# State-space scan: gates in the output weights, D u and residual rows as TensorE products, copies on ScalarE

## The reference, cut to what matters

```python
h = _layernorm(x) * (1 + ca) + sa
xz = h @ W_in                       # halves: x_conv input, z
x_conv = silu(causal_conv(xz[:, :128]) + conv_b)      # "u" in the kernel
B_sel, C_sel, delta = split(x_conv @ W_xproj);  delta = softplus(delta)
state = exp(delta * A) * state + delta * B_sel * u    # 16 states a channel, over time
y = sum_n(state * C_sel)
y = y + x_conv * D_param
y = y * silu(z)
x = x + ga * (y @ W_out)            # ga: one row of 128 gates for each batch
```

## Time and profile before

| | |
|---|---|
| median of three runs | 1981.86 us |
| the profiled execution | 1981.38 us, its span 1979.6 us |
| mean granted clock of TensorE over the span | 0.908 of full |
| scan stage, first to last group's product | 1395.08 to 1643.64 us |
| busy over the span | PE 82%, DVE 61%, ACT 39%, POOL 65% |

### The profile page before, as it was taken

The page is one execution under the profiler, slowest core; times in us unless marked ns, Lnnn a source line. Parts: engine busy times, 40 slices in busy tenths (PEclk is TensorE's granted clock), DMA queues, the critical chain, the costliest instruction groups (busy, mean ns, idle before and its releaser), DMA issues. The chain is left out here.

```text
span 1979.6 us, 26522 instructions
## 1 busy us (share of the span) xinstructions
PE 1617.7 (82%) x9024; PEld 1115.1 (56%) x9024; DVE 1201.4 (61%) x2409; ACT 764.4 (39%) x1278; POOL 1288.5 (65%) x1091
## 2 busy tenths in 40 slices
PE   5799999999999999999999899998776765347670
PEld 3455656665567556676565787886333333236560
DVE  6876666667665666756661456664799997511124
ACT  2245444354443544434445333222866530102120
POOL 4588898789887898878888511100477775481516
PEclk7799999999999999999999999999988876577885
DMA  6223122112211222121210200000000002022213
GB/s 168 65 76 96 44 65 65 37 40 65 54 44 44 65 47 51 41 68 40 58 33 12 62 1 1 1 1 22 0 1 0 0 0 88 29 71 66 79 50 83
DMA packets 82740, 90.67 MB, mean 46 GB/s; under 512 B 12448, under 2 KB 52276, under 8 KB 82608
## 3 DMA queue, kind: packets, MB, share of 16 engines
q1 hardware_dynamic: 78512, 80.97, 16.6%
q0 software_dynamic: 4096, 8.02, 1.4%
HBM read 24.05 MB, written 14.68 MB: 20 GB/s over the span
## 5 line engine op out<-in xcount | busy, mean ns | idle before, releaser
L835 DVE CUSTOM_DVE_ANT_0 ring<-ring,mask 128x128 f32<-128x128 f32 (+7 forms) x512 | 383.8, 769 | 184.3 <-PE ring L697 183.8
L921 ACT ACTIVATE prob<-ring 128x512 f32<-128x512 f32 x576 | 315.2, 597 | 297.0 <-PE ring L712 293.2
L975 POOL TENSOR_TENSOR acc<-acc,prob 128x512 f32<-128x512 f32 x272 | 353.6, 1300 | 72.6 <-ACT prob L921 48.8
L728 PE MATMUL ps_o<-prob,v 128*64 128x256 f32 x2304 | 281.5, 386 | 4.2 <-issue 3.8
L697 PE MATMUL ring<-k,x 128*128 128x512 f32 (+3 forms) x768 | 249.6, 405 | 37.3 <-ACT prob L921 22.3
L711 PE MATMUL ring<-x,k 128*128 128x512 f32 x576 | 257.2, 447 | 25.0 <-DVE neg_m L835 15.7
L712 PE MATMUL ring<-x,k 128*128 128x512 f32 x576 | 229.1, 398 | 0.0
L697 PEld LDWEIGHTS ring<-k,x 128*128 128x128 f32 x768 | 136.4, 197 | 145.1 <-ACT prob L921 51.2
L728 PEld LDWEIGHTS ps_o<-prob,v 128*64 128x64 f32 x2304 | 154.0, 136 | 106.1 <-issue 38.4
L972 POOL TENSOR_TENSOR acc<-prob 128x512 f32<-128x512 f32 x144 | 184.1, 1279 | 7.9 <-ACT prob L921 6.6
L942 POOL TENSOR_TENSOR other<-other,sin 128x512 f32<-128x512 f32 x96 | 136.5, 1422 | 58.1 <-DVE other L814 57.6
(11 more groups left out here) (302 smaller groups left out, 3179.8 us busy)
## 6 DMA issues: line engine op xcount, KB each, us to landing
x<-other SPq DMA_DIRECT2D x256, 128.0 KB, 2.4
x<-rot SPq DMA_DIRECT2D x128, 128.0 KB, 2.4
slots_in<-zeros SPq DMA_DIRECT2D x2, 2048.0 KB, 8.7
slots_out<-wo SPq DMA_DIRECT2D x16, 256.0 KB
gate<-slots_in SPq DMA_DIRECT2D x11, 256.0 KB
e_w<-in_w SPq DMA_DIRECT2D x3, 704.0 KB, 6.7
x<-shift SPq DMA_DIRECT2D x128, 2.0 KB
first_h<-in_x SPq DMA_DIRECT2D x4, 512.0 KB, 4.9
```

The costliest lines, as they stand in the source:

```text
L728: mm = e.matmul(ps_o[s * D:(s + 1) * D, qb % 2 * 2 * P:(qb % 2 + 1) * 2 * P], v[g % 2][:, kb, :], prob[i % NPROB][:, s * 2 * P:(s + 1) * 2 ...
L835: e.tensor_tensor_reduce(ps, ps, mask_1[:, SEQ - n:SEQ], 1.0, -3.0 * NEG, ALU.add, ALU.min, neg_m[g % 2][:, c, h, qb % QPC:qb % QPC + 1]). ...
L921: e.activation(prob[i % NPROB][:, :], banks(("s2",) + key, BANK), ACT.Exp, scale=-1.0).then_inc(s2_exp.sem, 1)
L975: e.tensor_tensor(total[:, :], total[:, :], tile[:, :], ALU.add).then_inc(summed.sem, 1)
```

## The change

Two constants are made once on GpSimd: `w_gated`, the output weights times the gates for each batch, and `diag`, D_param on the diagonal of a 128x128 matrix. D*u is then added by products `diag` x u into `ps_y`, one for each half, ahead of the second fold sum of every batch. The output products use `w_gated`, and a product of the identity with x adds the residual rows in the same bank. ScalarE copies the bank to x. For batches 0 to 2 ScalarE copies `ps_y` to y and GpSimd multiplies by z as before; for batch 3 VectorE multiplies `ps_y` by z itself.

```diff
+        w_gated, diag = sb("w_gated", (P, BATCH, HID)), sb("diag", (P, P))
...
                 elif kind == "out":
                     b, n = key
-                    e.wait_ge(y_pool.sem, y_pool.at[key])
+                    e.wait_ge(gated_pool, 2)
+                    e.wait_ge(*y_made(key))
...
-                        mm = e.matmul(bank[:, j * HID:(j + 1) * HID], y[:, blk], w_out[:, :], start=True, stop=True)
+                        e.matmul(bank[:, j * HID:(j + 1) * HID], y[:, blk], w_gated[:, b, :], start=True, stop=False)
+                        mm = e.matmul(bank[:, j * HID:(j + 1) * HID], ident[:, :], x[:, b * TPB + n * 4 + j, :], start=False, stop=True)
...
                     if g == 0 and b:
-                        e.wait_ge(y_dve.sem, y_dve.at[b - 1, NC2 - 1])
+                        e.wait_ge(y_act.sem, y_act.at[b - 1, NC2 - 1])
+                    if g == 1:
+                        e.wait_ge(gated_pool, 2)
+                        for c in range(NC2):
+                            e.matmul(ps_y[c][:, :], diag[:, :], u[b % 2][:, c * BANK:(c + 1) * BANK], start=False, stop=False)
...                       # VectorE
-                elif kind == "y":
+                elif kind == "y" and key[0] == BATCH - 1:
...
-                        e.scalar_tensor_tensor(y[:, cc], u[b % 2][:, cc], dp[:, 0:1], ps_y[c][:, :], ALU.mult, ALU.add).then_inc(y_dve.sem, 1)
-                elif kind == "out":
...
-                    e.tensor_tensor(scaled[:, :, :], ps_w[turn[step] % 2][:, :].rearrange("p (j n) -> p j n", j=4),
-                                    gate_bc[:, b:b + 1, :].to_broadcast([P, 4, HID]), ALU.mult).then_inc(scale_dve.sem, 1)
+                        e.tensor_tensor(y[:, cc], ps_y[c][:, :], z[b % 2][:, cc], ALU.mult).then_inc(y_last.sem, 1)
...                       # ScalarE
-                        e.wait_ge(y_dve.sem, y_dve.at[b - 2, NC2 - 1])
+                        e.wait_ge(y_pe.sem, y_pe.at[b - 2, NG // SET - 1])
...
+                elif kind == "y" and key[0] < BATCH - 1:
+                    b, = key
+                    for c in range(NC2):
+                        if c < NC2 - 1:
+                            e.wait_ge(last_pe.sem, last_pe.at[b])
+                        else:
+                            e.wait_ge(y_pe.sem, y_pe.at[b, NG // SET - 1])
...
+                        e.activation(y[:, c * BANK:(c + 1) * BANK], ps_y[c][:, :], ACT.Copy).then_inc(y_act.sem, 1)
+                elif kind == "out":
+                    b, n = key
+                    tile = b * TPB + n * 4
+                    e.wait_ge(w_pe.sem, w_pe.at[step])
+                    e.activation(x[:, tile:tile + 4, :], ps_w[turn[step] % 2][:, :].rearrange("p (j n) -> p j n", j=4),
+                                 ACT.Copy).then_inc(add_act.sem, 1)
...                       # GpSimd
+            e.wait_ge(loaded, LATER * 16)
+            e.tensor_tensor(w_gated[:, :, :], gate_bc[:, :, :], w_out[:, :].rearrange("p (o n) -> p o n", o=1).to_broadcast([P, BATCH, HID]),
+                            ALU.mult).then_inc(gated_pool, 1)
+            e.tensor_scalar(diag[:, :], ident[:, :], dp[:, 0:1], None, ALU.mult).then_inc(gated_pool, 1)
...
-                elif kind == "out":
...
-                    e.tensor_tensor(x[:, tile:tile + 4, :], x[:, tile:tile + 4, :], scaled[:, :, :], ALU.add).then_inc(add_pool.sem, 1)
```

More of the change, by code:

```diff
@@ L1810, in selective_scan @@
         half = NG * P // 2
-        sel_in0, sel_in1, consts, a_exp, a_ready, sel_done, rstd_act, nmr_dve = (
-            sem(n) for n in ("sel_in0", "sel_in1", "const", "a", "a_neg", "sel", "rstd", "nmr"))
+        sel_in0, sel_in1, consts, a_exp, a_ready, sel_done, rstd_act, nmr_dve, gated_pool = (
+            sem(n) for n in ("sel_in0", "sel_in1", "const", "a", "a_neg", "sel", "rstd", "nmr", "gated"))
         x_norm = mark("x_norm")
         w_pe, x_pe, y_pe = mark("w_pe"), mark("x_pe"), mark("y_pe")
-        act, delta_dve, bu_dve, scan_dve, y_dve, scale_dve = (
-            mark(n) for n in ("act", "delta", "bu", "scan", "y", "scale"))
-        y_pool, du_pool = mark("y_pool"), mark("du")
+        act, delta_dve, bu_dve, scan_dve, y_act = (
+            mark(n) for n in ("act", "delta", "bu", "scan", "y"))
+        y_pool, y_last, du_pool = mark("y_pool"), mark("y_last"), mark("du")
         last_pe = mark("last_pe")
-        da_act, hc_pool, add_pool = mark("da"), mark("hc"), mark("add")
+        da_act, hc_pool, add_act = mark("da"), mark("hc"), mark("add")
         row_chain = Steps(nc, sems, "m_stats")
@@ L1851, in selective_scan @@
                 for c in range(NC2):
-                    for m in (y_dve, y_pool):
+                    for m in (y_act, y_pool) if key[0] < BATCH - 1 else (y_last,):
                         m.add(key + (c,))
             elif kind == "out":
-                scale_dve.add(key), add_pool.add(key)
+                add_act.add(key)
         def bank_read(step):
@@ L1864, in bank_read, with y_made @@
             return act.sem, act.at[past]
+        def y_made(key):
+            m = y_pool if key[0] < BATCH - 1 else y_last
+            return m.sem, m.at[key]
         def du_made(kind, b):
```

22 lines of the change are left out of this document (9 added, 13 removed).

## The result

The changed kernel takes 1984.69 us in the median of 19 runs (1982.80 to 1988.78), the kernel before 1981.86 in 19 beside it. The ratio is 1.0017, with a 95% interval of 1.0010 to 1.0024: 2.0 to 4.8 us slower, a difference that is clear of noise but small. The forecast was 1987, 5.4 more than before, in a range of 1976 to 1995.

What follows compares the result with a forecast made beforehand. VectorE sets the scan's pace while TensorE fills banks in time; after the change TensorE was to bound stretches. Terms 1.7 + 0.9 - 2.0 + 0.1 + 1.6 + 1.3 + 1.5 + 0.3 = +5.4 us: 1987, range 1976 to 1995.

Steps and rivals of the forecast that it cites:

- norm and outputs, groups 18 to 22: Batch 1's first groups: norm behind ScalarE's copies and doubled output products make TensorE the bound, 1.7 us later.
- norm and outputs, groups 34 to 38: Batch 2's first groups: the same delayed norm and doubled output products, 0.9 us later.
- batch 2's y and outputs (50 to 54): Batch 3's first groups, no norm behind the copies: VectorE's saved y sums and output steps gain 2.0 us.
- signs that I had named: Products of 18 to 22 and 34 to 38 wait 1 to 1.5 us; 26, 42 and 58 over 1 us each.
- ScalarE's place in the order: Batch ends: y copies delay norm, transposes and next fill; 1.30 us saved becomes 1.1 lost at 18, 0.3 at 34.
- Rival 3: Norm's hole on TensorE drops its clock for 4 to 8 us, adding about 3 us per batch: 1992; chance 0.22.
- Twice the output products: Output steps: identity products double TensorE's instructions, 2.1 us more a batch, so TensorE bounds groups 18 to 22 and 34 to 38.
- The diagonal: Two fp32 products ahead of each batch's second fold sum: costs of 0.1, 1.6, 1.3 and 1.5 us in batches 0 to 3.
- Rival 2: Added products hold TensorE's clock high; the diagonal costs 0.1, 0, -0.5 and 0.3: 1982.5 us; chance 0.18.
- The tail: End of the stage: 32 output instructions instead of 16, clock rising partway; last statistics 0.3 us later, bounds -0.5 and +1.5.
- Rival 1: VectorE keeps the pace in the scan stage: 7.4 us less and the tail's 0.3, 1974.8 us; chance 0.12.

Runs made afterwards that it cites:

- 1: Changed kernel with the y step of batches 0 to 2 placed behind the second norm and turn instead of ahead: 0.9975 of the kernel before.
- 7: Changed kernel with VectorE multiplying the PSUM sums by z for every batch, without ScalarE copies or GpSimd products of y: 0.9988 of the kernel before.
- 10: Kernel before with ScalarE copying ps_y to y in place of VectorE's step (u times D_param left out): 0.9987 of the kernel before.
- experiment 3: Changed kernel without the identity products of the output steps (residual rows left out): 0.9997 of the kernel before.
- 11: Kernel before with the identity products with x added to its output steps: 1.0005 of the kernel before.
- 2: Changed kernel without the products of the diagonal with u (u times D_param left out): 0.9997 of the kernel before.
- 5: Changed kernel run again without any edit, for a second trace: 1.0013 of the kernel before.
- 9: Kernel before run again without any edit, for a second trace: 1985.53 us in a single execution.
- experiment 8: Changed kernel with batch 3's y made as the others, ScalarE copying and GpSimd multiplying by z: 1.0016 of the kernel before.
- 4: Changed kernel with the diagonal's products moved from the second fold sum to ahead of the third sum's wait for GpSimd: 1.0011 of the kernel before.
- 6: Changed kernel with y behind norm and turn and the diagonal ahead of the third sum's wait: 0.9973 of the kernel before.
- 12: Changed kernel with y behind norm and turn, diagonal ahead of the third sum's wait, in batch 3 behind the first fold sum: 0.9956 of the kernel before.

## Why the prediction was right, and where its terms were off

The direction held, and the time lies well inside the range; the size came to about half: +5.4 forecast, +2.05 in the stage by the traces, +2.8 by the medians. The mechanism was the one named: work left VectorE, and its waits for fills in groups 2 to 63 rose from 8.95 to 19.31 us, 10.4 where I had said 12.5. VectorE was relieved of 6.4 us up to group 63's product (busy 227.1 us instead of 233.5), not of 7.4. Up to there the stage grew by 4.06 where the forecast had 5.1; the tail had the wrong sign. Step by step, in us of the stage:

| step | forecast | measured |
|---|---|---|
| diagonal, batch 0 | +0.1 | +0.1 |
| norm and outputs, groups 18 to 22 | +1.7 | +2.6 |
| diagonal, batch 1 (26) | +1.6 | +0.3 |
| third sum, batch 1 (30) | 0 | +0.2 |
| norm and outputs, groups 34 to 38 | +0.9 | +0.3 |
| diagonal, batch 2 (42) | +1.3 | -0.4 |
| third sum, batch 2 (46) | 0 | +0.2 |
| batch 2's y and outputs (50 to 54) | -2.0 | -1.9 |
| diagonal, batch 3 (58) | +1.5 | +2.6 |
| tail | +0.3 | -2.0 |

Term by term the misses add up to 8.4 us, more than the whole difference, and they cancel down to 3.4. So the mechanism of the first step was foreseen, but that the sum came out near is in part luck: the terms that depend on TensorE's clock missed either way. Of the signs that I had named, the waits at 18, 34 and 58 came, those over 1 us at 26 and 42 did not (0.36 and 0.37).

**ScalarE's place in the order** was right and is shown by experiments 1, 7 and 10. Its size in batch 1's groups was that of the walk (1.1) plus the low clock behind the hole: 2.2 at group 18. Rival 3 named this, and its mechanism happened in one batch of two. Read in windows of half a microsecond, the granted clock is 1.00 from 1469.00 to 1472.00, 0.77 from there to 1472.50 and 0.50 until it rises again in the window 1475.50 to 1476.00: 3.4 us low, where the rival had 4 to 8, so that it cost 1.1 and not 3. In batch 2's groups the clock stayed high through the same hole, and the product came 0.26 later where I had 0.3.

**Twice the output products** bound TensorE where I said (waits at 20, 21 and 37 that experiment 3 takes away, and that are not there in 11, where VectorE kept its work), but the stretch cost 0.4 and 0 more after group 18 and 34, not 0.6 each.

**The diagonal** is the term that was mis-sized in batches 1 and 2: I let its products and the sum behind them run at the clock that the earlier trace rows show, 3.4 plus 1.9. They ran high, 1.98 and 1.92 (1.91 of the first before the second could start, where I had 1.7):

```profile
1502.39 1.98 PE L1959 MATMUL m_ps_y<-m_u,m_diag 128*128 128x512 f32 x4 [1.02 <-POOL m_hc L2138]
...
1504.30 1.92 PE L1962 MATMUL m_ps_y<-m_hc,m_fold 128*32 128x512 f32 x16
```

Rival 2 had about these numbers (0 and -0.5, measured +0.3 and -0.4), for a reason that experiments 2, 10 and 11 do not bear out. The cost of an operation read at one clock doesn't stay with its place once the work ahead of it has changed. In batch 3 the products ran low (3.78) and the sum behind them took 2.05, and the wait of 58 was 2.54. Here the forecast's own figures did not give its term: 3.4 + 1.9 - 2.88 less 0.3 of room is 2.1, not 1.5.

**The tail** had the wrong sign. The structure was read rightly, but I kept the low clock until 1658 from the kernel before. In the changed kernel it rises about 4.5 us after the last sum begins. Windows (columns as in the earlier trace rows): two of the kernel before, whose sum starts at 1649.65, then those of the changed kernel, whose sum starts at 1658.86:

```profile
1653.00:1655.00 2.00, 1.40 (x9) 1.14 (x6) 0.75 (x1) 0.00 (x0) 1.56 (x2) 0.50 0.00 0
1655.00:1657.00 2.00, 2.00 (x11) 2.00 (x10) 0.69 (x1) 0.00 (x0) 0.72 (x2) 0.50 0.00 0
```

```profile
1662.00:1664.00 2.00, 2.00 (x14) 1.57 (x11) 0.69 (x1) 0.00 (x0) 0.00 (x0) 0.65 0.00 0
1664.00:1666.00 2.00, 2.00 (x20) 2.00 (x19) 0.40 (x2) 0.60 (x1) 0.00 (x0) 1.00 0.00 0
```

So 32 instructions take 4.3 us where 16 took 3.8, and where I had given them 6.4: that is 2.1 of the 2.3 us by which the tail missed. The chain behind them is one copy in place of a scaling and an add:

```profile
1664.97 0.60 ACT L2087 ACTIVATE first_h<-m_ps_w 128x512 f32<-128x512 f32 x1 [24.56 <-PE m_ps_w L1935]
...
1667.39 0.87 DVE L156 BATCH_NORM_STATS2 stats<-first_h 128x6 f32<-128x128 f32 x4 [0.49 <-ACT first_h L2087]
```

Why the clock rises early in the one and late in the other stays open. Either kernel repeats its own moment (experiments 5 and 9: 4.6 and 8.6 us after the sum's start). It isn't the hole of half a microsecond (8: 4.6 us with it), nor the number of output products (with the identity added to the kernel before, 11, the tail grew by 1.96, and its products ran low up to 9 us after the sum began), nor the changed tail as such: in experiment 10, with the old output steps, it rose after 5.1 us. Over all 14 traces it is 2.7 to 5.1 us in eleven and 8.6 to 9.2 in three, so the tail's gain of 2.0 can't be put down to the way the tail is built.

Rival 1, VectorE keeps the pace, was refuted. But most of what stood in its way was one place in a list: with y behind norm (1) the stage is 4.7 us shorter than before, in the middle 2.6 of the 7.4 us that it hoped for.

## What to carry to other kernels

When work moves to an idle engine, look at what stands behind it in that engine's order, not at the engine's load. ScalarE had 23 idle us in 63, and two copies of 0.6 us placed ahead of a preparation step cost more than the 1.3 us of VectorE that they saved, both times that such a step stood behind them (2.2 and 0.3 us net); in batch 2, with none behind, the saving stayed. Put such a step behind the last one that another engine waits for.

A hole of 2 us on TensorE can cost twice: its length and, in one of the changed kernel's two, 1.1 us by the low clock behind it. Added products can be laid into a hole: the diagonal's, laid into TensorE's wait for GpSimd, took the waits of 26 and 42 away (experiments 4 and 6), though part of the gain came back further on. Read an operation's duration together with the clock that it had.

## What the runs showed of the hardware

In two executions each of the two kernels, the granted clock changed at the same places of the work: the traces of experiments 5 and 9 repeat the first ones' waits within 0.02 us, though their stages start 0.3 and 2.3 us apart from the first, counted from the span's start. With other work ahead of them the same instructions met another clock (34's wait: 1.48, 3.55, 3.24 in the changed kernel, experiments 3 and 4). Two executions of the 14 (8 and 12) showed another pattern from the stage's first fill on, which took 0.76 and 0.77 us instead of 0.47, with 2.59 instead of 3.48 us ahead of group 1; experiment 8's was 1.04 us later at the last group than the changed kernel. So one trace of a version tells such small differences only within about 2 us (these 1.04 and the 0.9 ahead of group 0's product, an estimate from one trace), unless the waits ahead of its first groups agree with the other's.
